# Keys, queries and outputs stored by dimension with time innermost, and sums of eight terms made by adding halves

## The reference, cut to what matters

```python
q = silu(x @ Wq).reshape(b, n, h, hd)            # hd = 8
k = silu(x @ Wk).reshape(b, n, h, hd)
k = k * rsqrt(sum(k * k, -1) + 1e-12)            # key norms: a sum of 8 squares
def step(S, inp):                                # 256 steps, one after another
    Sd = a_t * S
    u  = v_t - k_t . Sd
    Sn = Sd + b_t * k_t (x) u
    return Sn, q_t . Sn
o = o * rsqrt(mean(o * o, -1) + 1e-6)            # output norms: a sum of 8 squares
x = x + ga * ((o * norm_w) @ Wo)                 # then layer norm, routing, experts
```

## Time and profile before

| | |
|---|---|
| runs | 491.4, 489.62, 487.44 us; median 489.62 |
| profiled execution | span 487.9 us; no other time of it is recorded |
| VectorE busy | 383.3 us, 79% of the span, 1166 instructions |
| TensorE busy | 377.1 us, 77% |
| ScalarE busy | 277.9 us, 57% |
| GpSimd busy | 263.1 us, 54% |

### The profile page before, as it was taken

The page is one execution under the profiler, slowest core; times in us unless marked ns, Lnnn a source line. Parts: engine busy times, 40 slices in busy tenths (PEclk is TensorE's granted clock), DMA queues, the critical chain, the costliest instruction groups (busy, mean ns, idle before and its releaser), DMA issues.

```text
span 487.9 us, 8633 instructions
## 1 busy us (share of the span) xinstructions
PE 377.1 (77%) x2505; PEld 325.1 (67%) x2505; DVE 383.3 (79%) x1166; ACT 277.9 (57%) x624; POOL 263.1 (54%) x325
## 2 busy tenths in 40 slices
PE   2967763956799978948779588699997779999970
PEld 1322312754678568938669578598997678999960
DVE  5778999999999999999979997749664224468624
ACT  3697967756474666766466353548454354555520
POOL 1127238999999678576772884022216663333340
PEclk9978995978889997987976869989999977999995
DMA  8177799990000019431000011341131122414006
GB/s 227 41 101 125 109 118 151 103 69 1 1 0 1 2 18 388 114 57 31 0 2 0 13 39 51 75 88 35 39 114 38 50 78 56 130 42 130 29 27 177
DMA packets 49309, 35.00 MB, mean 72 GB/s; under 512 B 10992, under 2 KB 45584, under 8 KB 49136
## 3 DMA queue, kind: packets, MB, share of 16 engines
q1 hardware_dynamic: 45424, 28.28, 30.7%
q0 software_dynamic: 3264, 5.92, 4.0%
q10 hardware_dynamic: 576, 0.26, 0.2%
HBM read 15.26 MB, written 10.27 MB: 52 GB/s over the span
## 4 chain that ended last, share of the span: by engine, by line
DVE 33%; PE 31%; POOL 13%; issue 11%; ACT 5%; DMA 2%; another core or an unknown queue 2%; ACTq 1%; SPq 0%; POOLq 0%; DVEq 0%
PE bank L839 12%; PE bank L854 5%; DVE U L1682 5%; DVE S L1695 5%; DVE p L1676 4%; DVE p L1689 4%; PE bank L650 4%; POOL big L950 2%; DVE big L1612 2%; PE bank L738 2%; DVE X L1614 2%; PE bank L593 1%; PE bank L654 1%; POOL X L918 1%
## 5 line engine op out<-in xcount | busy, mean ns | idle before, releaser
L1052 POOL DMA_INDIRECT placed_y<-Q,place x46 | 44.1, 958 | 101.9 <-DVE place L1888 38.1
L839 PE MATMUL bank<-Q,p 128*128 128x128 f32 x736 | 97.2, 281 | 2.2 <-ACT p L1399 2.2
L650 PE MATMUL bank<-prod_o,ID 128*128 128x128 f32 x512 | 75.4, 308 | 29.0 <-POOL prod_o L294 17.1
L839 PEld LDWEIGHTS bank<-Q,p 128*128 128x128 f32 x736 | 92.1, 197 | 2.6 <-ACT p L1399 2.4
L650 PEld LDWEIGHTS bank<-prod_o,ID 128*128 128x128 f32 x512 | 70.4, 219 | 31.8 <-POOL prod_o L294 20.3
L1210 ACT ACTIVATE p<-S,GAM 128x64 f32<-128x64 f32 x126 | 48.3, 410 | 65.4 <-DVE S L1695 64.6
L287 POOL TENSOR_TENSOR prod_o<-Q,ST 128x1024 f32<-128x1024 f32 x28 | 60.0, 2141 | 29.6 <-PE bank L654 17.1
L1399 ACT ACTIVATE p<-big 128x1024 f32 x46 | 48.5, 1057 | 44.4 <-PE bank L839 30.7
L1695 DVE TENSOR_REDUCE S<-p 128x64 f32<-128x320 f32 x126 | 56.6, 488 | 0.0
L1682 DVE TENSOR_REDUCE U<-p 128x32 f32<-128x288 f32 x128 | 53.0, 454 | 0.0
L1676 DVE TENSOR_TENSOR p<-S,bank 128x256 f32<-128x256 f32 x128 | 49.7, 423 | 0.7 <-ACT bank L1205 0.7
(11 more groups left out here) (253 smaller groups left out, 740.4 us busy)
## 6 DMA issues: line engine op xcount, KB each, us to landing
big<-in_L_ffn_w_dram SPq DMA_DIRECT2D x1, 4096.0 KB, 14.1
big<-big SPq DMA_DIRECT2D x16, 192.0 KB, 5.0
Q<-sorted_h SPq DMA_DIRECT2D x46, 64.5 KB
sorted_h<-ZERO SPq DMA_DIRECT2D x2, 1472.0 KB, 19.4
X<-in_L_attn_x_dram SPq DMA_DIRECT2D x8, 256.0 KB, 4.4
big<-big SPq DMA_DIRECT2D x16, 128.0 KB, 5.2
K<-placed_y SPq DMA_DIRECT2D x8, 256.0 KB
out_dram<-X SPq DMA_DIRECT2D x8, 256.0 KB, 2.3
```

Of the source, the lines that this page charges most:

```text
L650: pe.matmul(ps, ID[:, :], prod_o[:, k % 2, i, :], start=(i == 0), stop=False, skip_group_check=True)
L839: m = pe.matmul(bank[(1, 6)[g % 2] + k][:, c * P:(c + 1) * P], W1E[g % 2][:, f:f + P], XST[:, g % 3, :], start=True, stop=True)
L1052: pool.indirect_dma_start(placed_y[g // NF], bass.IndirectOffsetOnAxis(ap=place[:, g:g + 1], axis=0), YS[:, g % YR, :], None).then_inc(sem ...
```

## The change

`K_`, `Q_` and the second copy `KE` become `[P, 2, 8, 128]`: slice, dimension, time. Every view of them follows. What was a reading across the storage order of `RAW` becomes a reading in its order (unit keys, squares, copied queries). Pair products step through time inside a chunk (4, 3, 2 or 1 neighbours) and write without gaps, where they stepped through the 8 dimensions. Weighing keys on GpSimd (L924) now reads the keys across their storage order, since its destination `X_` keeps its layout.

The sums over 8 dimensions that VectorE made with one reduction (key norms of half 0, pair products of slice 0 in three reductions, squared outputs of slice 1) become three additions of halves: 4 + 4 rows, 2 + 2, 1 + 1. The three multiplications of `multiply_pairs` no longer wait for each other.

```diff
-        K_ = [sb(f"K{h}", [P, N, HD]) for h in range(NHALF)]
-        Q_ = [sb(f"Q{h}", [P, N, HD]) for h in range(NHALF)]
+        K_ = [sb(f"K{h}", [P, NTIME, HD, P]) for h in range(NHALF)]
+        Q_ = [sb(f"Q{h}", [P, NTIME, HD, P]) for h in range(NHALF)]
...
-            engine.tensor_tensor(OV[s][h], K_[h][:, s * P:(s + 1) * P, :].rearrange("p t v -> p v t"),
+            engine.tensor_tensor(OV[s][h], K_[h][:, s, :, :],
                                  rn[:, h * P:(h + 1) * P].unsqueeze(1).broadcast_to([P, HD, P]), ALU.mult)\
...
+        def under(v):
+
+            return v.unsqueeze(1).broadcast_to([P, HD, P])
+
+        def in_chunks(rows):
+
+            return rows.rearrange("p d (n i) -> p d n i", i=C)
...
-                pool.tensor_tensor(slice_rows(X_[h], s)[:, :, HD:2 * HD], slice_rows(K_[h], s), over(w), ALU.mult)\
+                pool.tensor_tensor(slice_rows(X_[h], s)[:, :, HD:2 * HD], K_[h][:, s, :, :].rearrange("p d t -> p t d"), over(w), ALU.mult)\
...
-                    last = pool.tensor_tensor(t4, Q4[:, :, d:C, :], K4[:, :, 0:C - d, :], ALU.mult)
+                    last = pool.tensor_tensor(t4, Q4[:, :, :, d:C], K4[:, :, :, 0:C - d], ALU.mult)
...
-                if (h, s) == (0, 0):
-                    act.activation(slice_rows(K_[h], s), keys.rearrange("p d t -> p t d"), ACT.Square).then_inc(sem("ksq"), 1)
-                else:
-                    act.activation(key_squares(h, s), keys, ACT.Square).then_inc(sem("ksq"), 1)
+                act.activation(key_squares(h, s), keys, ACT.Square).then_inc(sem("ksq"), 1)
...
-                act.activation(slice_rows(Q_[h], s), RAW[h][:, :, 2, :].rearrange("p d t -> p t d"), ACT.Copy).then_inc(sem("q_raw", h), 1)
+                act.activation(Q_[h][:, s, :, :], RAW[h][:, :, 2, :], ACT.Copy).then_inc(sem("q_raw", h), 1)
...
+            def halve(terms, count):
+                return dve.tensor_tensor(terms[:, 0:count, :], terms[:, 0:count, :], terms[:, count:2 * count, :], ALU.add)
+
             def key_norms(h):
+                terms = key_squares(h, 0)
                 dve.wait_ge(sem("ksq"), h + 1)
-                yield from ask_root(dve.tensor_reduce(bank_vectors(h, 0)[0], slice_rows(K_[h], 0), AX_X, ALU.add))
+                yield from settle(halve(terms, HD // 2))
+                yield from settle(halve(terms, HD // 4))
+                yield from ask_root(dve.tensor_tensor(bank_vectors(h, 0)[0], terms[:, 0, :], terms[:, 1, :], ALU.add))
...
-                dve.tensor_tensor(slice_rows(K_[h], s), RAW[h][:, :, 0, :].rearrange("p d t -> p t d"), over(rn), ALU.mult)\
+                dve.tensor_tensor(K_[h][:, s, :, :], RAW[h][:, :, 0, :], under(rn), ALU.mult)\
...
-                K4 = slice_rows(K_[h], 0).rearrange("p (n i) d -> p n i d", i=C)
-                for d, T4 in enumerate(front_pairs(), start=1):
-                    yield from settle(dve.tensor_tensor(T4, K4[:, :, d:C, :], K4[:, :, 0:C - d, :], ALU.mult))
+                K4 = in_chunks(K_[h][:, 0, :, :])
+                for d, (t4, _) in enumerate(key_pairs(), start=1):
+                    ins = dve.tensor_tensor(t4, K4[:, :, :, d:C], K4[:, :, :, 0:C - d], ALU.mult)
+                yield from settle(ins)
+
+            def pair_sums(h):
+                return bank[6 - h][:, 0:SCH * C * (C - 1) // 2]
+
+            def add_pairs(h):
+
+                terms = key_terms()
+                yield from settle(halve(terms, HD // 2))
+                yield from settle(halve(terms, HD // 4))
+                yield from settle(dve.tensor_tensor(pair_sums(h), terms[:, 0, :], terms[:, 1, :], ALU.add))
...
-                    T4 = front_pairs()[d - 1]
-                    sums = bank_vectors(h, 0)[0][:, 0:SCH * (C - d)].rearrange("p (n i) -> p n i", n=SCH)
-                    yield from settle(dve.tensor_reduce(sums, T4, AX_X, ALU.add))
+                    first = SCH * sum(C - e for e in range(1, d))
+                    sums = pair_sums(h)[:, first:first + SCH * (C - d)].rearrange("p (n i) -> p n i", n=SCH)
...
                 dve.wait_ge(sem("sqo"), 2 + h + 1)
-                last = dve.tensor_reduce(ms[:, h * P:(h + 1) * P], SQO[1][h], AX_X, ALU.add)
+                yield from settle(halve(SQO[1][h], HD // 2))
+                yield from settle(halve(SQO[1][h], HD // 4))
+                last = dve.tensor_tensor(ms[:, h * P:(h + 1) * P], SQO[1][h][:, 0, :], SQO[1][h][:, 1, :], ALU.add)
```

More of the change, by code:

```diff
@@ L211, in adaln_block @@
                for h in range(NHALF)] for s in range(NTIME)]
-        YG = [[K_[h][:, s * P:(s + 1) * P, :].rearrange("p t d -> p (t d)").rearrange("p (n d) -> p n d", n=HB)
+        YG = [[K_[h][:, s, :, :].rearrange("p d t -> p (d t)").rearrange("p (n d) -> p n d", n=HB)
                for h in range(NHALF)] for s in range(NTIME)]
-        OV = [[Q_[h][:, s * P:(s + 1) * P, :].rearrange("p t d -> p (t d)").rearrange("p (v t) -> p v t", v=HD)
-               for h in range(NHALF)] for s in range(NTIME)]
+        OV = [[Q_[h][:, s, :, :] for h in range(NHALF)] for s in range(NTIME)]
         XG = [X[:, :, :].rearrange("p (b s) d -> p s b d", s=NTIME)[:, s, :, :] for s in range(NTIME)]
@@ L268, in bank_weights, with group_times @@
             return rows[:, :, (g - PG) * GC * C:(g - PG + 1) * GC * C]
+        def group_times(tile, g):
+            first = g % (NG // NTIME) * GC * C
+            return tile[:, g // (NG // NTIME), :, first:first + GC * C]
         def make_products(engine, g, h):
@@ L285, in make_products @@
                     engine.wait_ge(sem("kept", hh), g + 1)
-            q = Q_[h][:, times, :].rearrange("p (n i) k -> p k n i", n=GC).unsqueeze(4).broadcast_to(full)
+            q = group_times(Q_[h], g).rearrange("p k (n i) -> p k n i", n=GC).unsqueeze(4).broadcast_to(full)
             engine.tensor_tensor(slot[:, 0:HD, :, :, :], q, states.unsqueeze(3).broadcast_to(full), ALU.mult)
@@ L331, in key_squares @@
         def key_squares(h, s):
-            rows = slice_rows(K_[h], s)
-            return rows.rearrange("p t d -> p (t d)").rearrange("p (d t) -> p d t", d=HD)
+            return K_[h][:, s, :, :]
         def part(k, i):
@@ L771, in sum_output_squares @@
                 for v in range(HD):
-                    m = pe.matmul(norm_sums()[:, h * P:(h + 1) * P], ID[:, :], SQO[0][h][:, :, v], start=(v == 0), stop=(v == HD - 1))
+                    m = pe.matmul(norm_sums()[:, h * P:(h + 1) * P], ID[:, :], SQO[0][h][:, v, :], start=(v == 0), stop=(v == HD - 1))
                 m.then_inc(sem("norms_ps"), 1)
@@ L933, in decay_keys @@
                     pool.wait_ge(sem("qk_ready"), NHALF + h + 1)
-                    dst = slice_rows(K_[h], s)
-                pool.tensor_tensor(dst[:, times, :], slice_rows(K_[h], s)[:, times, :], over(ce)[:, times, :], ALU.mult)\
+                    dst = K_[h][:, s, :, :]
+                pool.tensor_tensor(dst[:, :, times], K_[h][:, s, :, times], under(ce)[:, :, times], ALU.mult)\
                     .then_inc(sem("k_decayed", h), 1)
@@ L967, in decay_queries @@
                 pool.wait_ge(sem("qk_ready"), j + 1)
-                q = slice_rows(Q_[h], s)
-                link(pool.tensor_tensor(q, q, over(vectors[2]), ALU.mult))
+                q = Q_[h][:, s, :, :]
+                link(pool.tensor_tensor(q, q, under(vectors[2]), ALU.mult))
                 pool.wait_ge(sem("qk_evac"), j + 1)
@@ L1660, in _ @@
                 now(decay_factors(h, 0))
+                now(add_pairs(h))
                 for d in range(1, C):
```

41 lines of the change are left out of this document (16 added, 25 removed).

## The result

The changed kernel takes 494.04 us, the median of four runs (493.35 to 494.65), beside 489.81 us for the kernel before in its four runs there. The ratio of the runs is 1.0089, with a 95% interval of 1.0047 to 1.0131: 4.2 us slower, where 2.0 us less was forecast. The profiled execution took 494.65 us, its span is 492.9 us.

The account below looks back on a forecast made before the run. VectorE's own work was taken to bound the kernel up to 300 us. Front +0.6, loop -2.1 and expert stage -0.5 made -2.0 us, a median of 487.6; the 8-in-10 range was 484.0 to 491.5.

Parts of the forecast that it names:

- Key norms, half 0: In the front, additions of 1.42 us replace a 1.23 us reduction; VectorE ends 0.66 us late, ScalarE 0.98.
- Unit keys, the scaled outputs: In the front, L1536 goes to 1.22 us, minus 0.7; in the expert stage, L246 takes 0.79 us less.
- single words: In the front's pair products on VectorE, 256 elements in runs of one word, priced like a reading across, add 0.19 us.
- Pair sums, "192 elements less, minus 0.2": In the front, reductions of 768, 512 and 256 elements become additions of 768, 384 and 192, saving 0.2 us.
- GpSimd's chain in half 0: In the front, GpSimd starts 0.98 us late and L924 costs 0.54 more; L1612 starts at 47.6, half 0 1.5 later.
- The front: From the key norms to the first recurrence product: half 0 loses 1.5 us, half 1 gains 0.9; net loss 0.6.
- Loop, "the blocks take 5.1": In the loop, GpSimd's query blocks fall from 6.07 to 5.1 us and VectorE's wait of 0.6 goes; loop gains 2.1.
- The gain of the unit keys: In the loop, VectorE gains two unit keys, 2 x 0.75 = 1.5 us, with no wait under them.
- Behind the loop, -0.5: In the expert stage, ScalarE's issue and the matmul at 317.52 come 0.54 us earlier; -0.5 us (0 to -1).
- Rival A: In GpSimd's products at distances 1 to 3, short runs make GpSimd the bound: +5.3 us, 494.9; chance 8%.

Follow-up runs that it names:

- hold: The changed kernel, but GpSimd's weighting of each half's keys in the front waits until VectorE has added that half's pair products; ratio to before 1.0086.
- pe_sums: The changed kernel, with the front's pair products summed by TensorE against the identity instead of by VectorE; ratio to before 1.0064.
- before_halves: The kernel before, in its own layout, with pair products written by dimension and added by halves in three instructions; ratio to before 1.0089.
- one_reduction: The changed kernel, with each half's pair products summed by one reduction of 1536 numbers instead of three additions by halves; ratio to before 1.0031.

## Why the prediction was wrong

- **Key norms, half 0**: right. From the mark at 28.73 us (29.60 after), L1478 started 2.54 us later; forecast 2.55. The wait for the roots was 0.41 us.
- **Unit keys, the scaled outputs**: right, 1219 and 1218 ns. The pair products of half 0 took 2.08 us (2.15 before), so single words cost nothing that shows.
- **Pair sums, "192 elements less, minus 0.2"**: the step that failed. It priced the additions by their elements, took the price from rows where VectorE was alone or had one input in SBUF, and put their meeting with GpSimd at nothing, though it saw that in half 1 GpSimd's weighting "lies beside them". They cost 7.1 and 4.5 us. With GpSimd away, 768, 384 and 192 elements cost 0.96 + 0.56 + 0.37 = 1.9 (half 1 of *hold*). From the mark to the first substitution this makes +4.2 us (21.52 against 17.34) instead of +1.5, and from there to that of half 1 +1.0 (22.03 against 21.01) instead of -0.9. A row of before had the warning: L1612, two inputs in SBUF, took 2.10 us at 46.07 with GpSimd's L935 beside it, and 1.80 in the second half. I used its start and not its length, and didn't weigh the rule of the Trainium skill that is named above.

```profile
45.92 0.63 POOL L935 TENSOR_TENSOR big<-K,sm 128x256 f32<-128x256 f32 x1
```

- **GpSimd's chain in half 0**: right in its parts. The weighted keys took 2.52 us (forecast 2.5) and ended 18.56 us after the mark (forecast 18.87); but VectorE was not there yet. The front is +5.0 us instead of +0.6.
- **Loop, "the blocks take 5.1"**: the second step that failed. The rate came from another kind of instruction (L924, where one operand repeats a number eight times), and was used for two tensors. Blocks of 6.88 us (256 products of single words at 1.15 us where they took 0.73, 512 at 1.51 where they took 1.28), and L979 and L946 at 2.37 instead of 1.96, brought waits of 2.4 and 2.1 us, where the forecast had none. The gain of the unit keys (1.5) is there: -0.6 + 4.5 - 1.5 = +2.4, measured +2.5.
- **Behind the loop, -0.5**: right in sign, too small. To the issue of the first output transfers, the part that it worked out, it is 0.8 us (11.61 to 10.84 from the loop's end). By ratio and marks together, the kernels of the new layout had 1.3 to 3.2 us less behind the loop than before (pe_sums none), before_halves 0.4 more; a ratio is good to some 0.3%, so single values mean little. In one_reduction VectorE is 1.4 us earlier at the end of its second product of the outputs (13.01 in place of 14.37 us from the loop's end); the rest is open.
- **Rival A** named 494.9 us, near what was measured. Its mechanism is there in part: short runs made GpSimd's blocks dearer (6.88 us; it had 7.3), and VectorE waits in the loop, 4.5 us and not 7.3. But two thirds of the loss (5.0 of 7.5) are in the front, which it took as the forecast did, so that its time comes near is luck.

## What to carry to other kernels

Before an operation of VectorE with two inputs in SBUF (or a plain copy between SBUF tensors) replaces a reduction or one with an input in PSUM, look at what GpSimd does in the same microseconds: its price is then not that of its elements alone, but includes the rest of GpSimd's instruction, and here at times the transfer issues and the product that stood behind them. A price taken from the trace holds only for the same number of tensors read and the same kind of repetition. When a helper engine gets slower, try to take its result up a step later: here one changed number gave back 2.8 to 3.2 us.

## What was not expected of the hardware

- VectorE and GpSimd take turns by whole instructions, in both directions: 384 numbers at 2.69 us beside products of 2.34, at 1.50 beside products of 1.15, and GpSimd loses 0.3 us to each of VectorE's additions (2.65 in place of 2.34).
- A GpSimd product behind four transfer issues kept an addition out for 4.41 us in all, and in another arrangement for 3.38; issues with nothing behind them for none (0.55).
- On GpSimd, a repeated vector is only cheap if each number serves neighbours (1.96 us against 2.34 for the whole vector repeated), and one tensor with itself costs 1.89. Single words at a distance make 256 products 1.15 us for two tensors, and 0.64 for one.
- A reduction by dimension, 1536 numbers 768 bytes apart, takes 2.72 us on VectorE, and 1.74 where they are neighbours.
